# A decoder layer: norms and query halves moved to GpSimd, last weight signs moved into cross attention, turned probabilities handled in pairs, scores 12 units ahead and transposes 4

## What is computed

```python
x = _layernorm(x + _L0_attn_ref(x, W_K, W_Q, W_V, W_O))          # causal, 16 heads of 128
x = _layernorm(x + _L0_xattn_ref(x, ctx_2048, ctx_2048, gamma))  # 8 heads, no weights
x = _layernorm(x + _L0_ffn_ref(x, W_g, W_u, W_d))
...
qk = jnp.einsum('bhdq,bhdl->bhql', qh, kh) * scale               # cross attention, contraction 64
sm = jax.nn.softmax(qk, axis=-1)
ret = jnp.einsum('bhql,bhdl->bhdq', sm, vh)
...
xq = activation_quant(rms_norm(x))                               # FFN, weights taken as jnp.sign(w)
ternary_matmul(silu(ternary_matmul(xq, W_g)) * ternary_matmul(xq, W_u), W_d)
```

## Time and profile before

| | |
|---|---|
| median of 3 runs | 1445.02 us (1444.38 to 1447.54) |
| the profiled execution | 1445.03 us, its span 1443.1 us |
| TensorE busy | 1403.4 us, 97% |
| VectorE, ScalarE, GpSimd busy | 1113.6, 701.3, 655.3 us |
| self attention | up to about 950 us |
| last outputs of self attention, first scores | about 950 to 988 us |
| cross attention in its steady order | about 988 to 1202 us |
| FFN | from 1201.95 us |

### The profile page before, as it was taken

The page is one execution under the profiler, slowest core; times in us unless marked ns, Lnnn a source line. Parts: engine busy times, 40 slices in busy tenths (PEclk is TensorE's granted clock), DMA queues, the critical chain, the costliest instruction groups (busy, mean ns, idle before and its releaser), DMA issues.

```text
span 1443.1 us, 23688 instructions
## 1 busy us (share of the span) xinstructions
PE 1403.4 (97%) x6784; PEld 1146.1 (79%) x6784; DVE 1113.6 (77%) x2413; ACT 701.3 (49%) x1512; POOL 655.3 (45%) x523
## 2 busy tenths in 40 slices
PE   8899999999999999999999999979999999999998
PEld 7788888888888888888888888867888886655665
DVE  5677777877777777777787777778899877698846
ACT  3544445454444444454535444437888774333333
POOL 1434435244252543434524425255678783343434
PEclk9999999999999999999999999999999999999999
DMA  7476766757667667676675766776767944101101
GB/s 208 137 204 174 207 181 184 198 175 195 198 169 201 170 187 204 174 207 174 189 196 177 194 196 164 192 192 158 176 152 181 234 112 139 37 2 66 37 30 59
DMA packets 243885, 231.90 MB, mean 161 GB/s; under 512 B 102272, under 2 KB 212864, under 8 KB 243840
## 3 DMA queue, kind: packets, MB, share of 16 engines
q1 hardware_dynamic: 242688, 230.83, 58.3%
q10 hardware_dynamic: 1152, 0.52, 0.2%
HBM read 133.17 MB, written 90.24 MB: 155 GB/s over the span
## 4 chain that ended last, share of the span: by engine, by line
issue 44%; POOL 23%; PE 17%; DVE 7%; DMA 3%; ACT 2%; SPq 2%; POOLq 1%; DVEq 0%; ACTq 0%
POOL pT_lo L505 8%; PE bank L1653 7%; PE bank L1641 6%; POOL v_lo L503 5%; DMA xs<-rows_pair 2%; POOL xprobs L1116 2%; POOL ctx_halves L151 1%; POOL wqT_lo L498 1%; POOL wvT_lo L498 1%; DVE xpT_lo L1298 1%; DVE xneg_max L1291 1%; PE bank L1213 1%; ACT xprobs L1239 1%; PE bank L548 1%; PE bank L1173 1%
## 5 line engine op out<-in xcount | busy, mean ns | idle before, releaser
L690 ACT ACTIVATE probs<-probs,neg_max 128x128 f32<-128x128 f32 (+3 forms) x256 | 142.0, 556 | 379.5 <-DVE neg_max L819 379.5
L503 POOL TENSOR_TENSOR v_lo<-placed,v_hi 128x512 fp32r<-128x512 f32 x63 | 81.8, 1299 | 349.4 <-ACT v_hi L696 349.4
L505 POOL TENSOR_TENSOR pT_lo<-placed,pT_hi 128x1280 fp32r<-128x1280 f32 x63 | 186.3, 2958 | 0.0
L879 DVE SCALAR_TENSOR_TENSOR acc<-bank,prob_recip,acc 128x512 f32<-128x512 f32 x256 | 174.7, 745 | 5.5 <-PE bank L589 0.6
L1609 POOL TENSOR_TENSOR prod_lo<-prod,prod_hi 128x512 fp32r<-128x512 f32 x64 | 85.2, 1331 | 131.4 <-ACT prod_hi L1691 131.4
L831 DVE STREAM_TRANSPOSE turned<-probs 128x256 f32<-128x256 f32 (+1 forms) x384 | 113.9, 361 | 0.0
L789 DVE TENSOR_TENSOR qT_lo<-bank,qT_hi 128x512 fp32r<-128x512 f32 x64 | 44.2, 690 | 89.2 <-ACT qT_hi L678 89.2
L1116 POOL TENSOR_SCALAR xprobs<-xprobs,xprob_recip 128x512 f32<-128x512 f32 x128 | 86.6, 697 | 57.1 <-DVE xprob_recip L1302 57.1
L1653 PE MATMUL bank<-wdT_f32r,prod_hi 128*128 128x512 f32 x256 | 111.6, 436 | 0.8 <-POOL prod_lo L1609 0.6
L1239 ACT ACTIVATE xprobs<-bank,xneg_max 128x512 f32<-128x512 f32 x128 | 88.3, 690 | 43.3 <-DVE xneg_max L1291 40.3
L1213 PE MATMUL bank<-xpT_hi,values 128*128 128x512 f32 x256 | 103.3, 404 | 0.2 <-DVE xpT_lo L1298 0.2
(11 more groups left out here) (161 smaller groups left out, 3767.9 us busy)
## 6 DMA issues: line engine op xcount, KB each, us to landing
turned_scratch<-turned SPq DMA_DIRECT2D x64, 896.0 KB, 3.8
placed<-turned_scratch SPq DMA_DIRECT2D x252, 224.0 KB, 4.2
cp<-context_halves SPq DMA_DIRECT2D x64, 256.0 KB, 4.1
context_halves<-ctx_halves SPq DMA_DIRECT2D x16, 512.0 KB, 5.7
context_turned<-ctx_turned_block SPq DMA_DIRECT2D x32, 256.0 KB, 4.6
values<-context_turned SPq DMA_DIRECT2D x128, 64.0 KB, 2.3
xs<-rows_pair SPq DMA_DIRECT2D x60, 128.0 KB, 3.7
acc<-in_x_dram SPq DMA_DIRECT2D x16, 256.0 KB, 5.0
```

What stands on the lines that cost most here:

```text
L503: nc.gpsimd.tensor_tensor(v[par][1][:], landed_values(landing), v[par][0][:].bitcast(F32), ALU.subtract).then_inc(v_lo, 1)
L505: nc.gpsimd.tensor_tensor(pT[par][1][:], landed_probs(landing), pT[par][0][:].bitcast(F32), ALU.subtract).then_inc(p_lo, 1)
L690: nc.scalar.activation(probs[:, cols], probs[:, cols], ACT.Exp, bias=low[:, par, t:t + 1], scale=-1.0, accum_out=total[:, par, t:t + 1]).t ...
L879: nc.vector.scalar_tensor_tensor(out=acc[:, b * NT + t, :], in0=s_bank[t][:], scalar=recip[:, b, t:t + 1], in1=acc[:, b * NT + t, :], op0= ...
```

## The change

What it does, part by part:

- **Norms.** `apply_gpsimd` applies a norm in one GpSimd instruction (add of the negated mean, multiply), and `norm_whole_gpsimd` makes the negated mean. It takes the place of VectorE's `apply_norm` in cross attention and of the two instructions of `apply_beside`; `round_beside` adds a negative constant where it subtracted. Tile 0 of the first batch is normed by ScalarE.
- **Query halves.** Both halves are made by GpSimd (`queries`), at the end of the odd items, after the addition of `z_gamma`, for the pair that item m + 5 begins.
- **Signs of the last head.** Out of the end of self attention, into items 1, 3 and 5 of cross attention: `signs.turn` on VectorE and `signs.sign` on ScalarE stand at the end of the item's step, the latter ahead of `z_gamma`; SP stores them in items 2, 4 and 6. SP's loads of the three slices stand before item 4's loads, and the values of pairs 1 to 3 move in between the loads of items 2 and 3 and behind them.
- **End of self attention.** `zT` of batch 1 is split before the landed probabilities, two `add_outputs` come together, and a fourth score unit goes ahead of the last output product.
- **Cross attention.** A unit is now V(u), T(u + 4), S(u + 12), and `xpT_hi` and `xpT_lo` are made for two units at a time, 128 x 1024, at the odd units (`pair_bank`; the eight PSUM banks are one tensor).

```diff
+    def turn(self, nc, dve, m, h, raw):
+        dve.wait_ge(self.signed, h * 3 + m + 1)
+        dve.wait_ge(self.raw_loaded[m], h * (16 * self.E) + 16 * self.E)
...
+    def sign(self, nc, act, m, h):
+        act.wait_ge(self.turn_done, h * 3 + (m + 2))
+        nc.scalar.activation(out, x, ACT.Sign).then_inc(self.signed, 1)
...
+def norm_whole_gpsimd(nc, pool, norm, minus_half, n):
+    pool.wait_ge(norm.var_ready, n + 1)
+    nc.gpsimd.tensor_scalar(norm.minus_mean[:], norm.mv[:, :, 0], -1.0, 1.0, ALU.mult, ALU.mult).then_inc(norm.mean_ready, 1)
+    norm_gpsimd(nc, pool, norm, minus_half, n)
+def apply_gpsimd(nc, pool, norm, x, out, t, n):
+    if t == 0:
+        pool.wait_ge(norm.mean_ready, n + 1)
+        pool.wait_ge(norm.rstd_ready, n + 1)
+    return nc.gpsimd.tensor_scalar(out, x, norm.minus_mean[:, t:t + 1], norm.rstd[:, t:t + 1], ALU.add, ALU.mult)
...
-        loads(H - 1, 0, False)
-        exchange(FIRST + 2, 0, lambda: loads(H - 1, 1, False), landing=1)
-        loads(H - 1, 2, False)
+        exchange(FIRST + 2, 0, landing=1)
         exchange(FIRST + 3, 1)
-        keep_signs(H - 1, 0)
         sp.wait_ge(v_full, ITEMS)
         for item in range(2):
             rows.load_halves(sp, cross.cp, 0, item)
         cross.first_values(sp)
-        for m in (1, 2):
-            keep_signs(H - 1, m)
         rows.load_gamma(sp)
         cross.begin_sync(sp)
         rows.keep_halves(sp, halves, k, H - 1)
+        for m, name in enumerate(("wk", "wq", "wv")):
+            sp.wait_ge(w_turn[name], H)
+            signs.load_raw(sp, m, H - 1, raw[name][:])
         sp.wait_ge(o_added, H * B * NT)
...
         for unit in range(3):
             cross.scores(pe, unit)
+        pe.wait_ge(z_lo, ITEMS + 1)
+        cross.scores(pe, 3)
         output_product(FIRST + 3, 1)
-        for unit in range(3, 8):
+        for unit in range(4, 8):
             cross.scores(pe, unit)
...
-        sign(H - 1, 0)
         exps(FIRST + 3, 3)
         z_hi_of(0)
+        z_hi_of(1)
         halves_hi(FIRST + 2, 0, 1)
-        z_hi_of(1)
-        sign(H - 1, 1)
-        sign(H - 1, 2)
...
-        turn_ffn("wg", H - 1, 0)
         turn_v(FIRST + 3, 1)
         rows_of_scores(FIRST + 3, 3)
         turn_probs(FIRST + 3, 1)
         z_lo_of(0)
-        turn_ffn("wu", H - 1, 1)
         z_lo_of(1)
         add_outputs(FIRST, 0)
-        turn_ffn("wd", H - 1, 2)
+        add_outputs(FIRST + 1, 1)
+        z_lo_of(2)
         dve.wait_ge(o_added, (FIRST + 1) * NT)
         norm_stats(nc, dve, k, norm, norm_tiles(acc, 0), LN_EPS, 0, first=True)
-        add_outputs(FIRST + 1, 1)
-        z_lo_of(2)
         cross.first_queries_lo(dve)
-        for t in range(1, NT):
-            cross.apply_norm(dve, 0, t)
         add_outputs(FIRST + 2, 2)
         z_lo_of(3)
-        for unit in range(3):
+        for unit in range(4):
             cross.row_max(dve, unit)
         add_outputs(FIRST + 3, 3)
         cross.begin_vector(dve)
     cp: object
     begin_sync: object
     clear_values: object
...
-    S_AHEAD, PT_AHEAD = 10, NT - 2
+    def pair_bank(jt):
+        return banks[:, 4 + jt:6 + jt, :]
...
-        for pair in range(1, PAIRS):
-            source.load_values(sp, val, 0, pair)
         for h in (2, 3):
             sp.wait_ge(scores_full, (h - 1) * NT)
             load_item(sp, 0, h)
             load_queries(sp, 0, h)
+            source.load_values(sp, val, 0, h - 1)
+        source.load_values(sp, val, 0, PAIRS - 1)
...
+            if b == 0 and h - 1 in LAST_SIGNS:
+                signs.keep(sp, k, LAST_SIGNS.index(h - 1), H - 1)
...
-    def apply_norm(dve, b, t):
-    def queries_lo(pool, b, pair):
-        wait_apart(pool, k, x_hi, b * PAIRS + pair)
+    def first_norm(pool):
+        norm_whole_gpsimd(nc, pool, norm1, k.minus_half, 0)
+        pool.wait_ge(norm1.rstd_ready, 1)
+        nc.gpsimd.tensor_scalar(first_shift[:], norm1.mv[:, 0, 0:1], norm1.rstd[:, 0:1], -1.0, ALU.mult, ALU.mult).then_inc(first_shifted, 1)
+    def apply_norm(pool, b, t):
+        apply_gpsimd(nc, pool, norm1, tile_of(b, t), tile_of(b, t), t, b).then_inc(applied, 1)
+    def queries(pool, b, pair):
+        if b * PAIRS + pair > 1:
+            for i in range(2):
+                pool.wait_ge(xs_loaded[i], 32 * (b * PAIRS + pair - 1))
+        pool.wait_ge(applied, b * NT + pair)
+        nc.gpsimd.tensor_scalar(x_parts[:, 0, :].bitcast(F32R), tile_of(b, pair), 1.0, 1.0, ALU.mult, ALU.mult).then_inc(x_hi, 1)
+        pool.wait_ge(x_hi, b * PAIRS + pair)
...
-            if h % 2 == 0 and exists(m + 4, ITEMS):
-                nb, nh = ahead(b, h, 4)
-                queries_lo(pool, nb, nh // 2)
             if is_item(b, h, 1, 1):
                 quant.clear_steps(pool)
             if exists(m + 2, ITEMS):
                 normalise(pool, m + 2, (h + 2) % 4)
+            if h < NT and exists(b + 1, B):
+                apply_norm(pool, b + 1, h)
             if pair_ends(b, h):
                 wait_apart(pool, k, z_scaled, b * PAIRS + (h // 2 + 3))
                 tile = tile_of(b, h // 2)
                 nc.gpsimd.tensor_tensor(tile, z_gamma[:], tile, ALU.add).then_inc(z_added, 1)
+            if h % 2 == 1 and exists(m + 5, ITEMS):
+                nb, nh = ahead(b, h, 5)
+                queries(pool, nb, nh // 2)
             if normalises(b) and h == XH - 1:
-                norm_gpsimd(nc, pool, norm1, k.minus_half, b + 2)
-                pool.wait_ge(norm1.rstd_ready, b + 3)
+                norm_whole_gpsimd(nc, pool, norm1, k.minus_half, b + 2)
             quantise_beside(pool, m - QUANT_FROM)
...
     def turned_hi(act, u, jt):
-        act.wait_ge(pt_full, u + 1)
-        nc.scalar.copy(pT[0][:, jt, :], pt_bank[jt][:]).then_inc(pt_hi, 1)
+        act.wait_ge(pt_full, u + 2)
+        nc.scalar.copy(pT[0][:, jt:jt + 2, :], pair_bank(jt)).then_inc(pt_hi, 1)
...
-                if exists(u + PT_AHEAD, UNITS):
-                    turned_hi(act, u + PT_AHEAD, (j + PT_AHEAD) % NT)
-                if j == 0 and h % 2 == 0 and exists(m + 4, ITEMS):
-                    nb, nh = ahead(b, h, 4)
-                    queries_hi(act, nb, nh // 2)
+                if j % 2 == 1 and exists(u + PT_AHEAD, UNITS):
+                    turned_hi(act, u + PT_AHEAD - 1, j - 1)
+            if b == 0 and h in LAST_SIGNS:
+                signs.sign(nc, act, LAST_SIGNS.index(h), H - 1)
...
     def turned_lo(dve, u, jt):
-        dve.wait_ge(pt_hi, u + 1)
-        nc.vector.tensor_tensor(pT[1][:, jt, :], pt_bank[jt][:], pT[0][:, jt, :].bitcast(F32), ALU.subtract).then_inc(pt_lo, 1)
+        dve.wait_ge(pt_hi, u // 2 + 1)
+        nc.vector.tensor_tensor(pT[1][:, jt:jt + 2, :], pair_bank(jt), pT[0][:, jt:jt + 2, :].bitcast(F32), ALU.subtract).then_inc(pt_lo, 1)
...
-                if exists(u + PT_AHEAD, UNITS):
-                    turned_lo(dve, u + PT_AHEAD, (j + PT_AHEAD) % NT)
-                if j == 2 and exists(m + 2, ITEMS):
+                if j % 2 == 1 and exists(u + PT_AHEAD, UNITS):
+                    turned_lo(dve, u + PT_AHEAD - 1, j - 1)
+                if j == 0 and exists(m + 2, ITEMS):
                     reciprocals(dve, m + 2, (h + 2) % 4)
-                if j == 1 and h < NT and exists(b + 1, B):
-                    dve.wait_ge(norm1.rstd_ready, b + 2)
-                    apply_norm(dve, b + 1, h)
                 beside(b, h * NT + j)
+            if b == 0 and h in LAST_SIGNS:
+                m = LAST_SIGNS.index(h)
+                signs.turn(nc, dve, m, H - 1, source.nat[m][:])
...
-        self.nc.gpsimd.tensor_scalar(x, self.normed(0, t), norm.mv[:, t, 0:1], 1.0, ALU.subtract, ALU.mult).then_inc(self.beside_half, 1)
-        pool.wait_ge(self.beside_half, stage * NT + t + 1)
-        self.nc.gpsimd.tensor_scalar(x, x, norm.rstd[:, t:t + 1], 1.0, ALU.mult, ALU.mult
-                                     ).then_inc(norm.done if t == NT - 1 else self.beside_done, 1)
+        apply_gpsimd(self.nc, pool, norm, self.normed(0, t), out(0, t), t, 0).then_inc(norm.done if t == NT - 1 else self.beside_done, 1)```

The order on three engines. Numbers at the ends of names such as `cp_66` are buffers.

SP at the start of cross attention, before: from the last values of batch 0 to item 4 (`cp` are context halves, `xs` queries).

```order
L178 DMA values<-context_turned 32x4x128 x7
L184 DMA cp_66<-context_halves 64x1024 [waits xscores_full]
L184 DMA cp_66<-context_halves 64x1024
L1060 DMA xs_68<-rows_pair 64x512 [waits xn_lo,consts_ready]
L1060 DMA xs_68<-rows_pair 64x512
L184 DMA cp_67<-context_halves 64x1024 [waits xscores_full]
L184 DMA cp_67<-context_halves 64x1024
L1060 DMA xs_69<-rows_pair 64x512 x2
L156 DMA context_halves<-ctx_halves 128x1024 [waits ctx_split,consts_ready]
L184 DMA cp_66<-context_halves 64x1024 [waits xscores_full,consts_ready,o_added]
```

198 lines of the change are left out of this document (96 added, 102 removed).

## The result

The changed kernel takes 1488.5 us (median of 6 runs, 1485.8 to 1491.4), the kernel before beside it 1446.3 (6 runs): a ratio of 1.029, with a 95% interval of 1.027 to 1.031. It is 42 us slower. Forecast were 1471 and a range that ended at 1484: the direction was right, the size was not. The profiled execution has a span of 1489.3 us, 46.2 more than before.

| stretch (us) | before | forecast | after |
|---|---|---|---|
| S(16) starts at | 997.22 | 998.7 | 1000.17 |
| S(16) to S(40), three pairs with signs | 39.69 | 54.55 | 54.50 |
| S(40) to S(120), ten pairs | 138.86 | 147.6 | 161.91 |
| S(120) to the first gate product | 26.18 | 26.9 | 31.66 |

The account below looks back on a forecast made before the run. TensorE was taken to bound steady cross attention, with 11.6 us of waits. S(16) to S(120) adds 23.6 us, S(16) 1.5 and the tail 0.7: 25.8 over 1445.03, so 1471 us, range 1448 to 1484.

Parts of the forecast that it names:

- The start: Before item 4, SP begins at 970.9, needs 24.05 us, plus 3.7 to land: S(16) at 998.7, 1.5 us later.
- Term (2): Longer way to queries after a pair's last V: S starts at +10.3 instead of 8.38, a 1.9 us wait per pair.
- the shorter lead behind V end: From a pair's last V to the scores needing new queries: lead falls from 9.98 to 8.38 us, with 0.5 to spare.
- the norms' savings: Cross attention: GpSimd's 2 us less per item counted at nothing, inside 11.6 us of waits the longer pair already replaces.
- the three pairs with signs: Items 1, 3, 5: ScalarE's sign waits for VectorE, z_gamma comes 2.9 us later, S starts at +13.2 after V end.
- the ten pairs: S(40) to S(120): each pair of items takes 14.76 us with its wait for queries, together 147.6 us.
- rival B: Cross attention: the clock falls in every pair, ten pairs losing up to 1.4 us each: 1485 us; chance 0.12.
- term (6): Cross attention: pair operations, with 0.15 to 0.2 us saved per engine, and GpSimd's work until +8.65 counted at nothing.
- the tail: After S(120): one V less has been done by S(16), adding 0.7 us before the FFN's first gate product.
- 3.25 at the least: Query DMA landings take at least 3.25 us by the profile rows, so 3.7 is used, not the skill page's 2.3.
- rival C: Query landings take 2.3 us instead of 3.7, leaving a pair's wait at 0.5: 1451 us; chance 0.08.

Follow-up runs that it names:

- experiment 3: Changed kernel, with SP issuing the twelve last FFN weight loads in items 0, 2 and 4 behind each item's queries, not all before item 4's: 1482.3 us.
- experiment 9: Changed kernel with turned probabilities' halves copied per unit again, plus scores 10 units ahead and transposes 2, instead of 12 and 4: 1464.9 us.
- experiment 8: Kernel before, with only the norms changed: applied on GpSimd in one operation with the negated mean, rounding adding the negated constant: 1444.4 us, ratio 0.9983.
- experiment 2: Changed kernel, with ScalarE taking the sign behind z_gamma, not ahead of it, in items 1, 3 and 5: 1486.6 us.
- experiment 5: Changed kernel, with high and low halves of the turned probabilities made per unit again, one bank each, as before the change: 1474.0 us.
- experiment 1: Changed kernel, with GpSimd making both halves of the next queries before it waits for z_gamma and adds it: 1477.2 us.
- the order (without the rounding's move): Changed kernel with per-unit copies, leads 10 and 2, sign, weight loads and turned halves moved, and T and S ahead of V again: 1440.3 us.
- experiment 11: Changed kernel with per-unit copies, leads 10 and 2, and four moves: rounding ahead of the addition, sign behind z_gamma, weights late, turned halves kept later: 1454.8 us.

## Why the prediction was right and wrong

**Right.** The start: S(16) at 998.7 was 1000.17, waiting 7.6 us for queries behind SP's weight loads, which experiment 3 confirmed. Its terms missed by more, in both directions: SP began at 968.70 and not at 970.9, needed 27.2 us to the second xs for 24.05, and the landing took 4.1 for 3.7. Term (2) holds where nothing else is in the way (S(56) at +10.4 for +10.3). The direction, and that the shorter lead behind V end is one cause: experiment 9 takes the waits for queries and probabilities away. That the norms' savings are small: 2.5 us by the ratio of experiment 8, with an interval of 0.6 to 4.5.

**Right by luck, the three pairs with signs:** 54.55 us forecast, 54.50 measured, S at +12.65, +13.2 and +13.4 for +13.2. The forecast had TensorE wait for queries at the even items. It does not:

```profile
1012.25 0.73 PE L1212 MATMUL banks<-cp,xs 128*128 128x512 f32 x2 [2.41 <-ACT xprobs L1272]
...
1018.67 0.72 PE L1212 MATMUL banks<-cp,xs 128*128 128x512 f32 x2
```

S(24), the second row, has no wait, nor have S(32) and S(40); their second xs landed in 2.3 to 2.4 us. TensorE waits for exponentials at S(21), S(29) and S(37) (5.3 us), for queries of the odd items at S(28) and S(36) (3.4 us) and at T (1.5 us). The first of these the forecast had inside another wait, and for the second it had no term. That agrees with experiment 2, where z_gamma ahead of the sign gave 2 or 3 us for 8.7.

**Wrong, the ten pairs:** 161.9 us for 147.6. I split each pair at S(n + 3), which stands 0.35 us behind V end.

- S(n) to S(n + 3): forecast 4.8 each, 48 in all, measured 54.0. Four pairs stand at 5.9 to 6.4 us and one, with slips and no slow matmul, at 5.2. This is rival B, the falling clock: it came in four of the ten pairs of this execution and cost 5.4 us. I gave it 0.12 and priced it as all or nothing.
- S(n + 3) to S(n + 8): forecast 9.95 each, 99.5 in all, measured 108.0. The last two pairs, at 13.1 and 12.0, are 5.2 us of it. There GpSimd's rounding stands between the queries and the probabilities:

```profile
1191.05 1.29 POOL L1145 TENSOR_TENSOR rows_pair<-acc,rows_pair 128x512 fp32r<-128x512 f32 x1
1192.31 0.71 POOL L1492 TENSOR_SCALAR scaled<-xhat,steps_per_unit 128x512 f32<-128x512 f32 x1
1193.11 1.94 POOL L1495 TENSOR_SCALAR xq<-scaled 128x512 bf16<-128x512 f32 x1
1195.14 2.70 POOL L1151 TENSOR_SCALAR xprobs<-xprobs,xprob_recip 128x512 f32<-128x512 f32 x4
```

  and T waits 3.56 us at 1197.89. The other eight pairs take 10.36 each, 3.3 us more in all; in them z_gamma starts 0.5 us later than the +1.9 of the forecast, on average, and at +3.0 where the exponential ahead of it was late.

So the step that failed is term (6), "at nothing". I had GpSimd's probabilities end at +8.65, after T wants them at +8.0, and put this "inside the same wait". Ahead of S(48) they end at +10.9. It is the first wait and holds S too; and I took the GpSimd work of an even item as queries and probabilities alone, where a square root (1.0), an application (0.8) or the rounding (2.7) can stand between. The other half of the same term, that pair operations cost nothing because "both have room", was the larger mistake: 14.5 us by experiment 5, in the late z_gamma, the held exponentials and the tail. I had sized them right (1.00 and 1.22 us for 1.0 and 1.2), but looked at their sum and not at what is queued behind each, nor at the ring that they close: 3.57 us for two units where TensorE needs 3.21 (experiment 1).

**Wrong, the tail:** 5.5 us for 0.7. V waits for the low half 1.36, 0.39 and 0.72 us (before: once, 0.19 us). The second stands behind ScalarE's table load of 1.28, the first behind a maximum that VectorE takes only after a long subtraction and a transposition, and from 1216.6 to 1225 the clock is at 0.70. With single copies the tail is 27.8.

**The landing.** Rows of `xs` have a median of 3.8 us after the change, 3.7 before. But these medians mix two kinds, and the "3.25 at the least" of the prediction holds in the chain alone: the shortest rows of the kernel before are 2.22 us. In the ten pairs the second xs of the even item, on which the forecast wait hangs, landed in 2.3 to 4.1 us, 2.9 on average; 3.7 was too long for it, and rival C was partly right. It is not seen in the time, as T waits first in most pairs.

**The undoings in a row:** single copies to 1474.0, the leads to 1464.9, four moves to 1454.8, the order (without the rounding's move) to 1440.3. Together they take back more than the 42 us. Each share holds in this order only.

## What to carry to other kernels

Work on an engine with idle time is not free: ask of each operation what stands behind it in its queue and who waits for that. Two short operations can be better than one long one, because the ring's own work passes between them; here that was worth 1%. Besides each engine's sum, add up every ring that goes from one engine to another and back: with the queries first it set the pace, while VectorE was busy for 75% and ScalarE for 67% of the ten pairs. And before one moves an operation earlier, its buffer should be free by then. When a lead behind a join is shortened, add up all the work of every engine from the join on, in its program order, with the rarest items too.

## What the hardware showed that I had not expected

**The clock and the wait ahead of it.** In the changed kernel waits of 1.93 us (at 1070.14) and 1.92 (1132.84) and one of 1.32 followed by 0.64 (1148.80) were followed by matmuls at the lower level; those of 1.50, 1.48 and 1.29 were not. With the scores computed three times, waits of 1.82 and 1.90 us at the same places left the clock alone. But so did waits of 1.93 and 1.91 us there with the weights late, where no matmul was added:

```profile
1064.52 0.66 PE L1226 MATMUL banks<-ident,xprobs 128*128 128x128 f32 x4 [1.93 <-POOL xprobs L1152]
1064.93 0.71 PE L1213 MATMUL banks<-cp,xs 128*128 128x512 f32 x2
...
1066.18 0.60 PE L1226 MATMUL banks<-ident,xprobs 128*128 128x128 f32 x4
1066.53 0.71 PE L1213 MATMUL banks<-cp,xs 128*128 128x512 f32 x2
```

The same wait of 1.93 us is followed by the lower level in one kernel and by the full clock in another, so its length does not decide alone. Whether matmuls that nobody needs, ahead of a wait, buy clock stays open: the run with them had the median of the changed kernel.

**A slip that is no wait.** Where V needs a half that comes just in time, the views list no wait, but the first matmul is 0.1 to 0.2 us longer: in experiment 11 from V(28) to V(107) it took 0.50 us or more where VectorE's half had ended at most 0.19 us before its start (48 times), and 0.45 or less where it had ended at least 0.24 us before (32 times). With seven of the eight steps of a pair at 1.66 to 1.80 us instead of 1.60 to 1.69, this makes up the 6 us that V's place cost in ten pairs (the seven steps lose 8.5, the eighth gives 2.5 back). The pitch of the starts shows it, the list of waits does not.
